# Written-out loops, and a multiply-add, an add and a relu in place of a test and a multiply, in a fused vision-and-text block on one core

## The chip, the core and the metric

The kernel runs on one core of a Trainium2 chip. Its engines are TensorE (PE; its weight loads are listed apart as PEld), VectorE (DVE), ScalarE (ACT), GpSimd (POOL) and SyncE (SP), which issues all DMAs here. Each engine has its own program and its own queue, and they wait for one another by semaphores. The metric is the device time of one launch in microseconds, median of the runs; lower is better. Before the change it is 5894.83 us.

## What is computed

For each of 8 images a tokenizer turns 518x518 pixels into 1024 tokens of width 128; 77 text tokens are appended, so L = 1101. An attention with 8 heads of width 64 and a causal mask follows, and then a second attention with 8 heads of width 16, in which every row keeps only its 16 largest logits:

```python
h = concatenate([tok(x), txt], axis=1)              # (8, 1101, 128)
h = h + causal_attn(layernorm(h))                   # softmax over tril, 8 heads x 64, plus its input
h = h + sparse_attn(layernorm(h))
# sparse_attn, after x + depthwise conv(x) and the projections of q, k, v (8 heads x 16):
logits = einsum('bmd,bpd->bmp', q * scale, k)
_, idx = lax.top_k(logits, 16)
attn = softmax(einsum('bmd,bmkd->bmk', q * scale, gather(k, idx)), axis=-1)
out = einsum('bmk,bmkd->bmd', attn, gather(v, idx)) @ wo_w.T + wo_b
```

Softmax over 16 chosen logits equals exp over all 1101 of them, set to zero where the logit isn't chosen, divided by the sum of what is left. The kernel does it so, with no gather.

## The kernel before

**Stages.** The program is a pipeline over images. Stage c (0 to 8) does the tokens and the causal attention of image c and the sparse attention of image c - 1. So stage 0 has causal work alone, stages 1 to 7 have both, and stage 8 has sparse work alone. A stage with both runs `tokens(c)`, five calls of `a_round`, `output(c)` and `projections(c)`. A round p (0 to 3) takes two heads of each attention in 18 steps, one step for each row tile of 128 tokens (9 tiles, 2 heads). The steps' order on PE and ACT is a list written out by hand (`step_events`). The last two steps' leftovers are carried into the next round, so rounds 1 to 3 begin with work of the round before.

**A sparse tile, engine by engine.** PE computes the logits into PSUM (L620). DVE takes the 8 largest (L1100), negates the first for the exp (L1105), replaces the 8 in a copy `A` by NEG (L1116), takes the next 8 (L1120) and replaces those by NEG too (L1125). ACT computes `E1 = exp(logits - max)` (L892). POOL turns `A` into a 0/1 mask by a test for NEG (L510) and multiplies it with `E1` in place (L515). Two steps later PE transposes `A` in blocks of 128 columns (L600, in groups of four into one of two PSUM banks), ACT copies each group to `PT` (L839, and L842 for the last block, 77 wide), PE sums `PT` with the values (L701), ACT copies these sums (`split`, L862) and PE joins them (L709). ACT's exp of a tile stands behind the `split` copy in ACT's queue, and PE's logits of the next tile wait for that exp.

**A causal tile.** PE computes scores (L672, with the mask added in PSUM at L680 or L667), DVE takes the row maximum (L1064), ACT the exp into `PB` (L903). PE transposes `PB` (L600 as well), the same two lines copy it (slot 1 of `PT`), and PE sums it with the values (L727).

**Loops and registers.** Stages 1 to 7 are one loop over c (a `Fori`), and within each stage rounds 1 and 2 and 3 are a loop over p, on every engine. Round 0 stands before that loop, written out. Stage 0 and stage 8 stand outside the loop over c, but their rounds 1 to 3 are loops too. In a loop the values that semaphores are compared with, and some addresses, come from registers, computed by register instructions in each engine's queue. PE's inner loop of stages 1 to 7 closes at L795, its loop over c at L791, those of stages 0 and 8 at L787 and L802.

**hold.** Many waits go through `hold`, which waits and then increments a counter that nobody waits for in the rounds.

Of the kernel before, what the change touches and what calls it, by code (L numbers as in the profile page):

```python
# [29 lines left out]
NP = HA // 2  # L30
HF, DF = 8, 16
TOK_EPS, EPS = 1e-3, 1e-5
NEG = -3.0e38
MASK = -1.0e9
# [129 lines left out]
def build(nc, x, txt, conv_w, conv_b, gamma, beta, dense_w, dense_b, W_in, b_in, W_out, b_out,  # L164
# [7 lines left out]
    with ctx:  # L172
# [167 lines left out]
        def hold(eng, s, value, counter):  # L340

            eng.wait_ge(s, value)
            eng.sem_inc(counter, 1)  # L343

# [7 lines left out]
        def _(sp):  # L352
# [64 lines left out]
            def cycle(c, first, last):  # L417

                sp.wait_ge(h_free, c + 1)
                sp.dma_start(H[0:TXT, NT - 1, :], txt[c]).then_inc(txt_loaded, 16)  # L420
                with sp.Fori(0, NP) as p:

                    sp.wait_ge(wp_free, c * NP + (p + 1))
                    for s in range(3):
                        sp.dma_start(Wp[:, s, :, :], win_v[p, s]).then_inc(wp_loaded, 16)
# [15 lines left out]
            cycle(0, True, False)  # L441
            with sp.Fori(1, B - 1) as c:
                cycle(c, False, False)
# [6 lines left out]
        def _(pool):  # L450
# [44 lines left out]
            def weights(c):  # L495


                wait_copied(pool, "FV", c - 1)
                pool.sem_inc(held_g, 1)
                with pool.Fori(0, NP) as p:  # L500
                    for k in range(STEPS):
                        if k in (0, 3):

                            hh = k // 3
                            hold(pool, weighed, sparse_tile(c, p, hh * NT) + 1, held_g)
                            nc.gpsimd.tensor_copy(Vh[:, hh, :, 0:DF + 1], Vf[:, :, 2 * p + hh, :]
                                                  ).then_inc(v_ready, 1)

                        hold(pool, cut16, sparse_tile(c, p, k) + 1, held_g)
                        nc.gpsimd.tensor_scalar(A[:, k % 3, :], A[:, k % 3, :], NEG, None, ALU.is_equal  # L510
                                                ).then_inc(marked, 1)

                        pool.wait_ge(logit_free, sparse_tile(c, p, k) + 2)
                        hold(pool, marked, sparse_tile(c, p, k) + 1, held_g)
                        nc.gpsimd.tensor_tensor(A[:, k % 3, :], A[:, k % 3, :], E1[:, k % 2, 0:L], ALU.mult  # L515
                                                ).then_inc(chosen, 1)

            halos(0)
            with pool.Fori(1, B) as c:
                halos(c)  # L520
                weights(c)
# [15 lines left out]
        def _(pe):  # L537
# [248 lines left out]
            a_round(0, 0, False, True, False)  # L786
            with pe.Fori(1, NP) as p:  # L787
                a_round(0, p, False, True, True)
            a_round(0, NP, False, True, True)
            projections(0, True)  # L790
            with pe.Fori(1, B) as c:  # L791
                tokens(c)
                sparse_inputs(c)
                a_round(c, 0, True, True, False)
                with pe.Fori(1, NP) as p:  # L795
                    a_round(c, p, True, True, True)
                a_round(c, NP, True, True, True)
                output(c)
                projections(c, False)
            sparse_inputs(B)  # L800
            a_round(B, 0, True, False, False)
            with pe.Fori(1, NP) as p:  # L802
                a_round(B, p, True, False, True)
# [5 lines left out]
        def _(act):  # L809
# [23 lines left out]

            def copy_turned(bank, slot, q0, tiles):

                short = tiles[-1] == NT - 1
                full = len(tiles) - short
                if full:
                    last = nc.scalar.copy(PT[:, slot, 128 * q0:128 * (q0 + full)], bank[:, 0:128 * full])  # L839
                if short:  # L840
                    o = 128 * (q0 + full)
                    last = nc.scalar.copy(PT[0:LAST, slot, o:o + 128], bank[0:LAST, 128 * full:128 * full + 128])  # L842
                last.then_inc(turn_free, 1)
# [90 lines left out]
            a_round(0, 0, False, True, False)  # L934
            with act.Fori(1, NP) as p:
                a_round(0, p, False, True, True)
            a_round(0, NP, False, True, True)
            projections(0)
            with act.Fori(1, B) as c:
                tokens(c)  # L940
                a_round(c, 0, True, True, False)
                with act.Fori(1, NP) as p:
                    a_round(c, p, True, True, True)
# [3 lines left out]
            a_round(B, 0, True, False, False)  # L947
            with act.Fori(1, NP) as p:
                a_round(B, p, True, False, True)
# [5 lines left out]
        def _(dve):  # L955
# [221 lines left out]
            a_round(0, 0, False, True, False)  # L1177
            with dve.Fori(1, NP) as p:
                a_round(0, p, False, True, True)
            a_round(0, NP, False, True, True)  # L1180
            projections(0)
            with dve.Fori(1, B) as c:
                tokens(c)
                a_round(c, 0, True, True, False)
                with dve.Fori(1, NP) as p:
                    a_round(c, p, True, True, True)
# [3 lines left out]
            a_round(B, 0, True, False, False)  # L1190
            with dve.Fori(1, NP) as p:
                a_round(B, p, True, False, True)
# [25 lines left out]
```

## Time and profile before

| | |
|---|---|
| median of 3 runs | 5894.83 us (5883.47 to 5908.94) |
| profiled execution, from first to last instruction | 5921.3 us |
| mean granted TensorE clock | 0.855 |
| PE busy | 4872.7 us, 82% |
| DVE busy | 4044.9 us, 68% |
| POOL busy | 3189.5 us, 54% |
| ACT busy | 2745.0 us, 46% |
| stage 0 | to about 612 us |
| stages 1 to 7 | to about 5459 us, some 690 us each |
| stage 8 | to the end, about 460 us |

Of the profiled execution the page gives the span; no other time of it is known, and the span is above all three runs. A busy share is an average over the stages, and a wait counts only where the waiting engine is the one that everything else waits for. A granted clock of 1.00 stands for 2.4 GHz and 0.50 for 1.2 GHz; values between are mixtures over time. In the timeline an entry in brackets is the engine's idle time just before the instruction and what ended it; "issue" means that nothing that the profile shows was waited for.

### The profile page before, as it was taken

To read this page: it belongs to the slowest core of one execution; us is meant where nothing else is said; L and a number is where in the kernel's file an instruction comes from. 1 tells how busy PE (TensorE), PEld (TensorE's weight loads), DVE (VectorE), ACT (ScalarE), POOL (GpSimd) and SP (SyncE) were. 2 spreads that over 40 slices of the span, in tenths; PEclk is the share of its full clock that TensorE was granted. 3 is DMA by queue.
4 is the path that set the end of the run, shared out by engine and by line. 5 is a ranking of instruction groups with operands and counts; after the bars stand their busy time and mean duration, and the time that the engine had idled before them with its cause. 6 is when DMAs were issued, how large, how long until landed. Compare 5 with 4: busy or idle time off the path is not lost. (4 is left out here: it accounts for less than half of the span.)

```text
span 5921.3 us, 104393 instructions
## 1 busy us (share of the span) xinstructions
PE 4872.7 (82%) x33480; PEld 3298.2 (56%) x33928; DVE 4044.9 (68%) x6958; ACT 2745.0 (46%) x5521; POOL 3189.5 (54%) x1495
## 2 busy tenths in 40 slices
PE   5999699887988688886998879886988879884777
PEld 3666565555555555564555645555555555553444
DVE  1111487766888488775778578884878668883887
ACT  1222255544555355553555445552555435552444
POOL 1000176653766176663666357661767447762887
PEclk8555798998999899898889989997999989996666
DMA  3020301003020300103020120203010030003000
GB/s 49 2 28 0 47 3 29 3 5 48 3 30 2 51 2 9 24 5 48 2 30 2 28 26 3 30 2 52 3 22 9 5 48 3 3 2 48 1 0 4
DMA packets 221648, 104.95 MB, mean 18 GB/s; under 512 B 183616, under 2 KB 198544, under 8 KB 221072
## 3 DMA queue, kind: packets, MB, share of 16 engines
q1 hardware_dynamic: 221072, 97.68, 11.1%
q8 instruction: 311, 5.10, 0.4%
q14 instruction: 265, 2.17, 0.1%
HBM read 78.98 MB, written 18.67 MB: 16 GB/s over the span
## 5 line engine op out<-in xcount | busy, mean ns | idle before, releaser
L510 POOL TENSOR_SCALAR A<-A 128x1101 f32<-128x1101 f32 x576 | 1732.6, 3008 | 1652.8 <-DVE A L1125 1651.6
L839 ACT COPY PT<-causal_ps 128x512 f32<-128x512 f32 (+3 forms) x1984 | 1064.8, 561 | 1216.9 <-PE causal_ps L600 1213.3
L515 POOL TENSOR_TENSOR A<-A,E 128x1101 f32<-128x1101 f32 x576 | 1378.8, 2394 | 101.6 <-POOL A L510 98.3
L1100 DVE MAX8 top<-logit_ps 128x8 f32<-128x1101 f32 x576 | 753.9, 1309 | 546.6 <-PE logit_ps L620 544.2
L600 PE MATMUL causal_ps<-ident,A 128*128 128x128 f32 (+1 forms) x5184 | 926.6, 313 | 18.2 <-POOL A L515 17.7
L727 PE MATMUL out_ps<-qk,PT 128*128 128x64 f32 x5760 | 875.7, 300 | 24.4 <-ACT PT L839 24.0
L672 PE MATMUL causal_ps<-qk 64*128 64x512 f32 (+3 forms) x1792 | 864.7, 596 | 11.7 <-ACT PB L903 6.6
L727 PEld LDWEIGHTS out_ps<-qk,PT 128*128 128x128 f32 x5760 | 808.7, 215 | 81.9 <-ACT PT L839 35.4
L1120 DVE MAX8 top<-A 128x8 f32<-128x1101 f32 x576 | 753.4, 1308 | 83.8
L600 PEld LDWEIGHTS causal_ps<-ident,A 128*128 128x128 f32 (+1 forms) x5184 | 693.2, 162 | 206.9 <-issue 148.7
L701 PE MATMUL out_ps<-PT,Vh 128*32 128x128 f32 (+1 forms) x10368 | 763.0, 302 | 38.8 <-DVE O L1088 14.9
L1116 DVE MATCH_REPLACE8 A<-top,logit_ps 128x1101 f32<-128x1101 f32 x576 | 746.1, 1295 | 0.0
L1125 DVE MATCH_REPLACE8 A<-top,A 128x1101 f32<-128x1101 f32 x576 | 743.5, 1291 | 0.0
L892 ACT ACTIVATE E<-logit_ps,negtop 128x1101 f32<-128x1101 f32 x576 | 686.9, 1193 | 61.7 <-DVE A L1116 60.7
L842 ACT COPY PT<-causal_ps 77x128 f32<-77x128 f32 x640 | 167.5, 262 | 854.6 <-PE causal_ps L600 854.0
L600 PE MATMUL causal_ps<-ident,PB 128*128 128x128 f32 (+1 forms) x2880 | 539.6, 307 | 0.0
L620 PE MATMUL logit_ps<-stack 128*128 (+2 forms) x1280 | 308.1, 334 | 251.2 <-ACT E L892 105.0
L1064 DVE TENSOR_REDUCE negmax<-causal_ps 128x1 f32<-128x128 f32 (+7 forms) x512 | 374.9, 743 | 161.9 <-PE causal_ps L680 161.9
L672 PEld LDWEIGHTS causal_ps<-qk 64*128 64x128 f32 x1792 | 324.0, 207 | 282.8 <-issue 256.5
L701 PEld LDWEIGHTS out_ps<-PT,Vh 128*32 128x32 f32 (+1 forms) x10368 | 271.5, 112 | 354.2 <-issue 186.6
L903 ACT ACTIVATE PB<-causal_ps,negmax 128x1024 f32<-128x1024 f32 (+7 forms) x576 | 454.9, 791 | 20.7 <-DVE negmax L1064 20.7
L709 PE MATMUL out_ps<-join,split 128*128 128x17 f32 x1152 | 240.8, 285 | 257.5 <-ACT split L862 257.5
(140 smaller groups left out, 3931.3 us busy)
## 6 DMA issues: line engine op xcount, KB each, us to landing
stack<-qk_parts SPq DMA_DIRECT2D x128, 288.0 KB, 20.2
X<-in_x SPq DMA_DIRECT2D x248, 121.5 KB, 4.1
qk_parts<-O SPq DMA_DIRECT2D x16, 864.0 KB, 4.8
Wp<-in_L_attn_W_in SPq DMA_DIRECT2D x96, 64.0 KB, 2.0
out<-OUTB SPq DMA_DIRECT2D x8, 512.0 KB
stack<-in_L_tok_conv_w SPq DMA_DIRECT2D x30, 64.0 KB, 2.4
X<-in_x SPq DMA_DIRECT2D x8, 108.0 KB
H<-in_txt SPq DMA_DIRECT2D x8, 38.5 KB
```

The costliest lines, as they stand in the source:

```text
L510: nc.gpsimd.tensor_scalar(A[:, k % 3, :], A[:, k % 3, :], NEG, None, ALU.is_equal).then_inc(marked, 1)
L515: nc.gpsimd.tensor_tensor(A[:, k % 3, :], A[:, k % 3, :], E1[:, k % 2, 0:L], ALU.mult).then_inc(chosen, 1)
L600: last = nc.tensor.transpose(bank[0:w, 128 * j:128 * j + 128], src, ident[:, :])
L672: last = nc.tensor.matmul(score_ps[:, c0:c1], q, qk[rows, 1, c0 - HALF * j:c1 - HALF * j], start=True, stop=not diagonal)
L701: last = nc.tensor.matmul(split_sums[32 * q:32 * q + 32, :], Vh[0:rows, h % 2, k, :], PT[0:rows, 0, 128 * k:128 * k + 128], start=(k < 4), ...
L727: last = nc.tensor.matmul(causal_sums[:, o:o + DK], PT[0:rows, 1, 512 * j + 128 * q:512 * j + 128 * q + 128], Vp[0:rows, k, DK * hh:DK * h ...
L839: last = nc.scalar.copy(PT[:, slot, 128 * q0:128 * (q0 + full)], bank[:, 0:128 * full])
L892: nc.scalar.activation(E1[:, n % 2, 0:L], logit_ps[:, 0:L], ACT.Exp, bias=negtop[:, n % 3:n % 3 + 1], scale=1.0).then_inc(logit_free, 1)
L1100: nc.vector.max(top[:, s, 0:8], logit_ps[:, 0:L]).then_inc(top8, 1)
L1116: nc.vector.match_replace(A[:, s, :], top[:, s, 0:8], logit_ps[:, 0:L], NEG).then_inc(cut8, 1)
L1120: nc.vector.max(top[:, s, 8:16], A[:, s, :]).then_inc(top16, 1)
L1125: nc.vector.match_replace(A[:, s, :], top[:, s, 8:16], A[:, s, :], NEG).then_inc(cut16, 1)
```

## The change

Four things are changed together.

- **Loops.** Every `Fori` of all five engines becomes a Python loop, so each queue is one straight piece of code. All semaphore values and addresses become constants, and the register instructions and branches are gone. PE's program grows from 1620 to 7943 printed rows.
- **hold** only waits; its increment is dropped.
- **The mask on POOL.** NEG becomes -2^127. The test `A == NEG` (one operation) becomes `A * 2^-27 + (-2^100)` (two operations in one instruction): exactly 0 where `A` is NEG, and -2^100 elsewhere. The multiplication with `E1` becomes an addition: `E1` where chosen, about -2^100 elsewhere.
- **The relu on ACT.** `copy_turned` now issues `activation` with Relu for slot 0 (sparse), which turns the large negative numbers into 0, and with Copy for slot 1 (causal).

```diff
-NEG = -3.0e38
+NEG = -2.0 ** 127
+FAR = -2.0 ** 100
...
             eng.wait_ge(s, value)
-            eng.sem_inc(counter, 1)
...
-                        nc.gpsimd.tensor_scalar(A[:, k % 3, :], A[:, k % 3, :], NEG, None, ALU.is_equal
+                        nc.gpsimd.tensor_scalar(A[:, k % 3, :], A[:, k % 3, :], FAR / -NEG, FAR, ALU.mult, ALU.add
                                                 ).then_inc(marked, 1)
...
-                        nc.gpsimd.tensor_tensor(A[:, k % 3, :], A[:, k % 3, :], E1[:, k % 2, 0:L], ALU.mult
+                        nc.gpsimd.tensor_tensor(A[:, k % 3, :], A[:, k % 3, :], E1[:, k % 2, 0:L], ALU.add
                                                 ).then_inc(chosen, 1)
...
             def copy_turned(bank, slot, q0, tiles):
+                kept = ACT.Relu if slot == 0 else ACT.Copy
...
-                    last = nc.scalar.copy(PT[:, slot, 128 * q0:128 * (q0 + full)], bank[:, 0:128 * full])
+                    last = nc.scalar.activation(PT[:, slot, 128 * q0:128 * (q0 + full)], bank[:, 0:128 * full], kept)
...
-                    last = nc.scalar.copy(PT[0:LAST, slot, o:o + 128], bank[0:LAST, 128 * full:128 * full + 128])
+                    last = nc.scalar.activation(PT[0:LAST, slot, o:o + 128], bank[0:LAST, 128 * full:128 * full + 128], kept)
...
-            with pe.Fori(1, B) as c:
+            for c in range(1, B):
                 tokens(c)
                 sparse_inputs(c)
                 a_round(c, 0, True, True, False)
-                with pe.Fori(1, NP) as p:
+                for p in range(1, NP):
                     a_round(c, p, True, True, True)
```

The other loops of SP, POOL, ACT and DVE are changed in the same way.

**PE at the end of a round's loop.** The order of PE's queue, in the kernel before, where the loop over p of stages 1 to 7 closes (an ISA row here is a register instruction):

```order
L720 ISA
L605 REGISTER_ALU [waits sum_free]
L727 MATMUL out_ps<-qk,PT 128x64 [waits turn_free]
L727 MATMUL out_ps<-qk,PT 128x64 x3
L795 REGISTER_ALU
L795 COMPARE_AND_BRANCH
```

The branch leads back to the loop's head, which reads:

```order
L620 ISA [waits logit_free]
L620 REGISTER_ALU
L620 MATMUL logit_ps<-stack 128x512
L620 ISA
L620 MATMUL logit_ps<-stack 128x512
L620 ISA
L620 MATMUL logit_ps<-stack 128x77
L605 ISA
L727 MATMUL out_ps<-qk,PT 128x64 [waits turn_free]
L727 MATMUL out_ps<-qk,PT 128x64 x3
```

The same place in the changed kernel, from the last sums of a round into the first logits of the next:

```order
L727 MATMUL out_ps<-qk,PT 128x64 x3
L620 MATMUL logit_ps<-stack 128x512 [waits logit_free]
L620 MATMUL logit_ps<-stack 128x512
L620 MATMUL logit_ps<-stack 128x77
L727 MATMUL out_ps<-qk,PT 128x64 [waits turn_free]
L727 MATMUL out_ps<-qk,PT 128x64 x3
```

The matmuls keep their order; the branch and the register instructions are gone, and the wait for the exp sits on the matmul itself.

**ACT near the end of a round.** ACT's queue in the kernel before, in a step with both kinds of work:

```order
L839 COPY PT<-causal_ps 128x512 [waits turn_done]
L850 REGISTER_ALU
L886 COPY tail<-causal_ps 128x77 [waits turn_done]
L850 REGISTER_ALU
L842 COPY PT<-causal_ps 77x128 [waits turn_done]
L850 REGISTER_ALU
L839 COPY PT<-causal_ps 128x512 [waits turn_done]
L862 COPY split<-out_ps 128x128 [waits split_done]
L889 REGISTER_ALU
L892 ACTIVATE E<-logit_ps,negtop 128x1101 [waits cut8,chosen]
```

And in the changed kernel:

```order
L840 ACTIVATE PT<-causal_ps 128x512 [waits turn_done] x2
L887 COPY tail<-causal_ps 128x77 [waits turn_done]
L843 ACTIVATE PT<-causal_ps 77x128 [waits turn_done]
L840 ACTIVATE PT<-causal_ps 128x512 [waits turn_done]
L863 COPY split<-out_ps 128x128 [waits split_done]
L893 ACTIVATE E<-logit_ps,negtop 128x1101 [waits cut8,chosen]
```

The order is the same; every copy into `PT` has become an ACTIVATE instruction, those of the causal work too, while `tail` and `split` stay COPY. ACT's whole queue holds one ACT_TABLE_LOAD in either kernel.

## Rows read from the trace of the kernel before

**Rows 1.** Busy time by stretch: bounds, length, engines, clock, DMA share, GB/s.

```profile
111.00:612.00 501.00, 461.94 (x1561) 310.15 (x1560) 85.81 (x232) 133.46 (x306) 4.71 (x32) 0.55 0.07 9
...
2887.00:3041.00 154.00, 139.71 (x915) 91.13 (x928) 117.29 (x189) 77.37 (x162) 97.73 (x38) 0.83 0.01 3
...
4935.00:5072.00 137.00, 121.16 (x930) 79.33 (x944) 116.80 (x188) 77.77 (x166) 98.21 (x39) 0.99 0.01 3
...
5569.00:5680.00 111.00, 85.46 (x562) 51.35 (x569) 98.85 (x130) 49.95 (x90) 97.40 (x37) 0.62 0.00 1
```

**Rows 2.** Waits of PE: who waited for whom, us in total, times, longest.

```profile
PE out_ps L709 <- ACT split L862: 257.5, 576, 0.5
...
PE logit_ps L620 <- ACT E L892: 105.0, 109, 4.6
PE logit_ps L620 <- issue: 61.5, 92, 3.4
...
PE out_ps L727 <- ACT PT L839: 24.0, 43, 1.0
PE causal_ps L600 <- POOL A L515: 17.7, 31, 1.7
...
PE causal_ps L666 <- ACT PT L839: 13.3, 56, 0.2
```

**Rows 3.** Timeline at the close of a round's loop, stage 3: start, us, engine, line.

```profile
2485.96 1.20 ACT L892 ACTIVATE E<-logit_ps,negtop 128x1101 f32<-128x1101 f32 x1
...
2486.84 1.00 PE L727 MATMUL out_ps<-qk,PT 128*128 128x64 f32 x8
...
2490.80 0.41 PE L620 MATMUL logit_ps<-stack 128*128 x2 [2.96 <-issue]
...
2491.05 1.50 PE L727 MATMUL out_ps<-qk,PT 128*128 128x64 f32 x8
```

**Rows 4.** Timeline of ACT: last and first causal exp around two changes of round, stage 3.

```profile
2199.72 1.10 ACT L903 ACTIVATE PB<-causal_ps,negmax 128x1024 f32<-128x1024 f32 x1
...
2223.53 0.37 ACT L903 ACTIVATE PB<-causal_ps,negmax 128x128 f32<-128x128 f32 x1 [0.29 <-DVE negmax L1064]
...
2487.88 1.10 ACT L903 ACTIVATE PB<-causal_ps,negmax 128x1024 f32<-128x1024 f32 x1
...
2516.27 0.37 ACT L903 ACTIVATE PB<-causal_ps,negmax 128x128 f32<-128x128 f32 x1 [0.30 <-DVE negmax L1064]
```

**Rows 5.** Timeline of a step of stage 3, from the last sparse sums to the join.

```profile
2595.07 0.41 PE L701 MATMUL out_ps<-PT,Vh 77*32 77x128 f32 x2
2595.17 0.59 ACT L839 COPY PT<-causal_ps 128x512 f32<-128x512 f32 x1 [0.68 <-PE causal_ps L600]
...
2595.98 0.40 PE L709 MATMUL out_ps<-join,split 128*128 128x17 f32 x2 [0.51 <-ACT split L862]
```

**Rows 6.** Groups of instructions by line: busy us, mean ns, idle before, releaser.

```profile
L510 POOL TENSOR_SCALAR A<-A 128x1101 f32<-128x1101 f32 x576 | 1732.6, 3008 | 1652.8 <-DVE A L1125 1651.6
L515 POOL TENSOR_TENSOR A<-A,E 128x1101 f32<-128x1101 f32 x576 | 1378.8, 2394 | 101.6 <-POOL A L510 98.3 <-ACT E L892 2.5 <-issue 0.9
...
L868 ACT ACTIVATE qk<-causal_ps,bqkv 128x1024 f32<-128x1024 f32 x32 | 35.7, 1115 | 91.9 <-PE causal_ps L630 91.9
...
L872 ACT COPY qk<-causal_ps 128x1024 f32<-128x1024 f32 x32 | 32.4, 1012 | 50.3 <-PE causal_ps L636 50.3
```

**Rows 7.** Timeline of stage 8: DVE and POOL from tile to tile.

```profile
5700.40 1.30 DVE L1100 MAX8 top<-logit_ps 128x8 f32<-128x1101 f32 x1
...
5706.20 1.30 DVE L1100 MAX8 top<-logit_ps 128x8 f32<-128x1101 f32 x1
...
5706.47 3.02 POOL L510 TENSOR_SCALAR A<-A 128x1101 f32<-128x1101 f32 x1
...
5712.28 3.01 POOL L510 TENSOR_SCALAR A<-A 128x1101 f32<-128x1101 f32 x1
```

**Rows 8.** Timeline of stage 3's tokens: the second layernorm.

```profile
2060.81 1.84 DVE L992 BATCH_NORM_STATS2 st<-H 128x6 f32<-128x128 f32 x9 [12.91 <-DMA H<-in_txt]
```

More of the change, by code:

```diff
@@ L420, in cycle @@
                 sp.dma_start(H[0:TXT, NT - 1, :], txt[c]).then_inc(txt_loaded, 16)
-                with sp.Fori(0, NP) as p:
+                for p in range(0, NP):
                     sp.wait_ge(wp_free, c * NP + (p + 1))
@@ L441, in _ @@
             cycle(0, True, False)
-            with sp.Fori(1, B - 1) as c:
+            for c in range(1, B - 1):
                 cycle(c, False, False)
@@ L499, in weights @@
                 pool.sem_inc(held_g, 1)
-                with pool.Fori(0, NP) as p:
+                for p in range(0, NP):
                     for k in range(STEPS):
@@ L514, in weights @@
                         hold(pool, marked, sparse_tile(c, p, k) + 1, held_g)
-                        nc.gpsimd.tensor_tensor(A[:, k % 3, :], A[:, k % 3, :], E1[:, k % 2, 0:L], ALU.mult
+                        nc.gpsimd.tensor_tensor(A[:, k % 3, :], A[:, k % 3, :], E1[:, k % 2, 0:L], ALU.add
                                                 ).then_inc(chosen, 1)
             halos(0)
-            with pool.Fori(1, B) as c:
+            for c in range(1, B):
                 halos(c)
@@ L790, in _ @@
             projections(0, True)
-            with pe.Fori(1, B) as c:
+            for c in range(1, B):
                 tokens(c)
@@ L794, in _ @@
                 a_round(c, 0, True, True, False)
-                with pe.Fori(1, NP) as p:
+                for p in range(1, NP):
                     a_round(c, p, True, True, True)
@@ L801, in _ @@
             a_round(B, 0, True, False, False)
-            with pe.Fori(1, NP) as p:
+            for p in range(1, NP):
                 a_round(B, p, True, False, True)
@@ L934, in _ @@
             a_round(0, 0, False, True, False)
-            with act.Fori(1, NP) as p:
+            for p in range(1, NP):
                 a_round(0, p, False, True, True)
@@ L938, in _ @@
             projections(0)
-            with act.Fori(1, B) as c:
+            for c in range(1, B):
                 tokens(c)
                 a_round(c, 0, True, True, False)
-                with act.Fori(1, NP) as p:
+                for p in range(1, NP):
                     a_round(c, p, True, True, True)
@@ L947, in _ @@
             a_round(B, 0, True, False, False)
-            with act.Fori(1, NP) as p:
+            for p in range(1, NP):
                 a_round(B, p, True, False, True)
@@ L1177, in _ @@
             a_round(0, 0, False, True, False)
-            with dve.Fori(1, NP) as p:
+            for p in range(1, NP):
                 a_round(0, p, False, True, True)
@@ L1181, in _ @@
             projections(0)
-            with dve.Fori(1, B) as c:
+            for c in range(1, B):
                 tokens(c)
                 a_round(c, 0, True, True, False)
-                with dve.Fori(1, NP) as p:
+                for p in range(1, NP):
                     a_round(c, p, True, True, True)
@@ L1190, in _ @@
             a_round(B, 0, True, False, False)
-            with dve.Fori(1, NP) as p:
+            for p in range(1, NP):
                 a_round(B, p, True, False, True)
```

## Prediction

> **What bounds the kernel now.** I read the stages first. PE is the engine to follow in stages 1 to 7: in a round of some 137 us it is busy 121 us at a clock of 0.99 [rows 1], while DVE, ACT and POOL are busy 117, 78 and 98 us. Stage 0 is PE too, at a clock of 0.55 and 92% busy [rows 1]. In stage 8 PE (85 of 111 us, clock 0.62), DVE (99) and POOL (97) are close together [rows 1]. So a microsecond counts in stages 0 to 7 if PE stands idle in it, and in stage 8 if it is taken from all three.
>
> Then PE's waits [rows 2]: 257.5 us before the join L709 for ACT's `split`, 105.0 us before the logits L620 for ACT's exp, 61.5 us before L620 with "issue", where nothing was waited for. Between images there is a second limit: the layernorm of the tokens waits 12.91 us for the text's DMA [rows 8], which stands in SP's queue behind the loads of `stack`. What makes PE quicker there is swallowed by that wait.
>
> **Loops written out.** At the close of the loop over p, PE ends L727 at 2487.84, the exp that L620 needs was over at 2487.16, and still L620 starts at 2490.80 [rows 3]: 2.96 us lost on the branch. Right behind it the same eight L727 take 1.50 us instead of 1.00 [rows 3]: the clock has fallen to its lower level (1.2 GHz) after the pause. The whole price is read by comparing two changes of round with the same work. From round 0 to round 1, where no branch is taken back, the last causal exp of a round and the first of the next lie 2223.53 - 2199.72 = 23.81 us apart; from round 2 to round 3 it is 2516.27 - 2487.88 = 28.39 us [rows 4]. I read all of stages 1 to 7 in this way: the 7 changes without the branch have 23.80 to 23.81 us, the 14 with it 28.08 to 30.19, mean 29.06. So 14 x (29.06 - 23.80) = **74 us** go. The loop over c closes 6 times with a pause of PE as well, but the wait for the text ends later [rows 8], so I count nothing; without that cover it would be about 2 us each, 12 in all. In stages 0 and 8 the branches show no such pause.
>
> **Registers and holds.** Of the 61.5 us of "issue" [rows 2], 14 x 2.96 = 41 are counted already. The rest, 20 us, are logits whose wait sat on a register instruction; I take 15. Where L620 waits for the exp, that instruction costs about 0.1 us more than a direct wait (0.15 us from the exp's end against 0.05 at L709 from `split`'s); 39 of the 109 waits lie before stage 8: 4 us. Elsewhere PE's and DVE's register instructions run ahead of the work: stage 0's written-out round and its looped rounds have the same length within 1%. Together **19 us** in stages 1 to 7.
>
> **POOL.** L510 costs 3.01 us, L515 2.39 us [rows 6]. No row has a multiply-add on POOL. From below, a two-input multiply of the same size costs 2.39; from above, two operations for one may double it, 6.02. I take 3.01, since it is the same instruction on the same tile, and the add like the multiply. In stages 1 to 7 POOL is idle a quarter of the time and PE waits for it 17.7 us in all [rows 2], 14.2 of them in stage 8, so nothing changes there for anything up to about 4.7 us.
>
> The Trainium skill (GPSIMD Engine Reference, section 3.1) says that a body with at most two operations per element is bound by its port at 1.03 cycles; an estimate by it is 1101 x 1.03 / 1.2 GHz = 0.95 us plus dispatch. By that, POOL's tile would fall from 5.8 to about 3.8 us and the sum would stay as it is, because DVE holds stage 8 at nearly the same pace. The trace bears such low figures out badly: one operation takes 3.01 us [rows 6].
>
> **ACT.** Each copy into `PT` becomes an ACTIVATE. The nearest rows, same shape and source: ACTIVATE 1115 ns, COPY 1012 ns [rows 6]. I take +0.10 us each; the range is 0 (if Relu and Copy are leaner than the biased form) to 0.10 on more of them than I count. No second table load is in the queue. ACT isn't full, so only exposed copies count. In most steps of stages 1 to 7 a causal copy stands before `split`: PE's sums L701 end at 2595.48, the copy at 2595.76, and L709 waits 0.51 us [rows 5]. I counted 306 of 504 joins with a wait of about 0.5 us, 114 with about 0.4 and 84 at the floor of 0.35: 306 x 0.10 + half of 114 x 0.10 = 36 us. L666 waits 56 times and L727 43 times for L839 [rows 2]: 10 us. A few L701: 4 us. Together **+50 us**. This is the term that speaks against the change.
>
> **Stage 8.** DVE goes from tile to tile in 5.80 us and POOL in 5.81 [rows 7]; the mean over the tiles is 111 / 18 = 6.2 [rows 1], since the loop through PE and ACT is slower when the clock is low. The written-out round 0 has 14 tiles in 84.5 us, rounds 1 to 3 in 86.7: 3 x 2.8 = 8 us for 18 tiles each. The dropped increments of `hold` shorten DVE's two gaps of 0.15 us and POOL's of 0.17 us by some 0.1 each: 8 us over the tiles that they bind. L620's direct wait gives 70 x 0.1 = 7 us, the slower ACT takes some 8 back. **-15 us**.
>
> **Sum.** 5921.3 - 74 - 19 + 50 - 15 = 5863 us for the profiled span, a factor of 0.990. The span is above the runs, so I apply the factor to the median: 5894.83 x 0.990 = **5837 us**.
>
> **Rivals.**
>
> *The clock moves more than the branch.* In steps 3 to 7 of a round PE's work is thin, and the clock falls there in most rounds, for 14 to 44 us. Round 1 of stage 4 took 154 us at 0.83, round 1 of stage 7 137 us at 0.99 [rows 1]: 17 us between worst and best. Against the best round all of them together lose 134 us. Shorter pauses should keep the clock up more often; if half of it goes, 5837 - 67 = 5770. The other way, if 10 more rounds are as bad as the worst, 6000. I see a reason for the first only, in the pauses that shrink by 0.1 us.
>
> *Only the pause goes.* The clock falls at the change of round all the same, so of 74 us only 41 come, and the slower copies are exposed about 20 us more, in the turn of the two PSUM banks. 5837 + 33 + 20 = 5890.
>
> *Code loading.* Straight code is longer than any loop body, and under the burst of `stack` loads a small transfer is late: the text's ends a wait of 12.91 us [rows 8]. If PE's code came as late in 7 stages by some 10 us, 5907. Against it: the code of stages 1 to 7 that isn't looped, tokens and round 0, is read the same way today, without a pause there. The Trainium skill (Runtime: NRT & Kernel Launch, Instruction fetch mechanics) calls sequential fetching mostly hidden and a taken branch a stall; by it this rival gives nothing and the sum stays.
>
> *POOL becomes the bound (slower than before).* If two operations cost twice the time, a tile on POOL takes 6.02 + 2.39 + 0.3 = 8.7 us, against 7.8 us per tile in stages 1 to 7 and 6.2 in stage 8. 504 x 0.9 + 72 x 2.5 = 634 us more than 5921, scaled about 6530. It decides from L510 above 3.3 us in stage 8 and above 4.7 us in the others (7.4 after the change, less 2.7).
>
> **How the numbers follow.** The forecast, 0.50, with a range of its own of 5800 to 5870. Half of the clock's loss gone, 0.20: 5770. Only the pause, 0.16: 5890. Code loading, 0.04: 5907. POOL, 0.06: 6530. Clock worse, 0.04: 6000. The range from 5750 to 5900 leaves out 0.10 above and a little below: if the copies cost nothing more and half of the clock's loss goes too, it is 5837 - 50 - 67 = 5720. Some 0.5% is what a measurement of this kernel can tell from no change; that is under 5865 for faster and over 5924 for slower. Faster holds the forecast nearly whole, the clock's gain and a part of the third case: 0.76. Same: 0.13. Slower: 0.11.
>
> **What would show it.** Right: no "issue" wait of more than 1 us before L620, changes of round of 24 us everywhere in stages 1 to 7, L839's 512 columns at 0.69 us instead of 0.59, L709's waits up by 0.1 us in three of five steps, L510 within 2.4 to 3.3 us. Wrong: PE idle with "issue" in straight code; POOL ending PE's waits before L600; round lengths that change in steps 3 to 7 with the clock, which would outweigh each of my terms.

## The result, and the profile after

The changed kernel takes **5693.2 us** in the median (5677.7 to 5703.7, 4 runs), the kernel before 5893.5 beside it. The ratio is 0.965, with a 95% interval of 0.960 to 0.970: faster by 200 us, where I had forecast 58, and outside my range (5750 to 5900). A second set of runs on another chip gave 0.964 [0.958, 0.970].

The profiled execution took 5677.7 us with a span of 5675.9. The span before was above all its runs, so the two spans differ by 245 us, more than the medians do. The account of the spans by part of the program:

| part, us | before | after |
|---|---|---|
| stage 0, first to last causal exp | 474.8 | 474.6 |
| 28 rounds of stages 1 to 7, first to last causal exp | 3214.6 | 3114.9 |
| 21 changes of round in stages 1 to 7 | 573.5 | 487.0 |
| between the stages | 961.3 | 952.3 |
| stage 8 with what leads into it | 576.9 | 527.4 |
| stretches at the low clock that touch the 28 rounds | 382 | 177 |

The first 120 us of each span, the same within 0.5 us, are not in the table. Of the low stretches 372 and 172 us lie inside the rounds.

The waits of PE after the change (who waited for whom, us in total, times, longest) answer to [rows 2]:

```profile
PE out_ps L709 <- ACT split L863: 259.4, 576, 0.5
...
PE logit_ps L620 <- ACT E L893: 101.3, 106, 4.3
...
PE out_ps L727 <- ACT PT L840: 25.9, 43, 0.8
...
PE logit_ps L620 <- issue: 16.4, 84, 0.2
```

"Issue" before L620 fell from 61.5 to 16.4 us, and its longest from 3.4 to 0.2: the pause at the branch is gone. The waits for the join hardly moved. At the same place as [rows 3], a close of a round in stage 3, the timeline now reads:

```profile
2400.82 1.00 PE L727 MATMUL out_ps<-qk,PT 128*128 128x64 f32 x8
2401.88 0.41 PE L620 MATMUL logit_ps<-stack 128*128 128x512 bf16 x2
2402.13 0.85 PE L727 MATMUL out_ps<-qk,PT 128*128 128x64 f32 x6
```

L620 follows at once, and the L727 behind it run at full clock.

The stretches (bounds, length, busy time of PE, PEld, DVE, ACT, POOL, clock, DMA share, GB/s) answer to [rows 1]: stage 0, an undisturbed round of stage 4, the slowest round of all (stage 4 too), and stage 8.

```profile
111.00:594.00 483.00, 443.21 (x1467) 294.46 (x1465) 84.64 (x228) 126.76 (x297) 4.71 (x32) 0.55 0.06 10
```

```profile
2812.00:2923.00 111.00, 101.05 (x777) 66.17 (x790) 99.74 (x163) 65.34 (x141) 54.00 (x32) 0.98 0.00 1
...
2946.00:3070.00 124.00, 114.81 (x775) 75.95 (x789) 99.00 (x161) 65.66 (x140) 53.94 (x32) 0.85 0.27 33
...
5562.00:5673.00 111.00, 81.47 (x591) 51.15 (x599) 90.46 (x122) 50.32 (x90) 60.10 (x36) 0.74 0.00 1
```

Stage 0 is as before, clock and all. In stage 8 POOL is busy 60 us of 111 instead of 97. DVE alone sets the pace there, 5.43 us from tile to tile (5302.61 to 5308.04), with POOL waiting for it:

```profile
5302.61 1.30 DVE L1101 MAX8 top<-logit_ps 128x8 f32<-128x1101 f32 x1
...
5308.04 1.30 DVE L1101 MAX8 top<-logit_ps 128x8 f32<-128x1101 f32 x1
```

```profile
5302.78 1.11 POOL L510 TENSOR_SCALAR A<-A 128x1101 f32<-128x1101 f32 x1 [1.65 <-DVE A L1126]
```

Last, the groups by line and shape (busy us, mean ns, idle before) for the changed operations, against [rows 6] and, for the copy, its own row of before:

```profile
L510 POOL TENSOR_SCALAR A<-A 128x1101 f32<-128x1101 f32 x576 | 642.2, 1115 | 2493.5 <-DVE A L1126 2493.5
```

```profile
L840 ACT ACTIVATE PT<-causal_ps 128x512 f32<-128x512 f32 x1664 | 939.0, 596 | 954.1 <-PE causal_ps L600 954.0
```

```profile
L839 ACT COPY PT<-causal_ps 128x512 f32<-128x512 f32 x1664 | 931.7, 588 | 1086.6 <-PE causal_ps L600 1083.4
```

The multiply-add takes 1.115 us where the test took 3.008, and the ACTIVATE 0.008 us more than the COPY.

### The profile page after: what moved, and what is told of

It is laid out like the page before. It is cut to its first block, busy times and chain, and to the rows that moved or that the text cites. A ratio compares the mean times of both kernels' runs of the same rounds, so it can differ in the third digit from the quotient of the medians.

```text
span 5675.9 us, 86247 instructions
## 1 busy us (share of the span) xinstructions
PE 4706.9 (83%) x33480; PEld 3201.5 (56%) x33928; DVE 4020.6 (71%) x6958; ACT 2745.6 (48%) x5521; POOL 2101.8 (37%) x1495
## 4 chain that ended last, share of the span: by engine, by line
PE 69%; DVE 10%; ACT 10%; DMA 5%; issue 4%; SPq 2%; POOL 0%; POOLq 0%; ACTq 0%; DVEq 0%
PE causal_ps L600 18%; PE causal_ps L672 14%; PE out_ps L727 13%; PE out_ps L701 7%; PE logit_ps L620 4%; ACT PT L840 4%; DMA H<-in_txt 4%; PE out_ps L709 3%; PE causal_ps L630 2%; ACT split L863 2%; DVE top L1101 2%; DVE A L1126 2%; PE causal_ps L680 1%; DVE top L1121 1%; DVE A L1117 1%
## 5 line engine op out<-in xcount | busy, mean ns | idle before, releaser
L840 ACT ACTIVATE PT<-causal_ps 128x512 f32<-128x512 f32 (+3 forms) x1984 | 1075.9, 569 | 1072.2 <-PE causal_ps L600 1071.8
L510 POOL TENSOR_SCALAR A<-A 128x1101 f32<-128x1101 f32 x576 | 642.2, 1115 | 2493.5 <-DVE A L1126 2493.5
L727 PE MATMUL out_ps<-qk,PT 128*128 128x64 f32 x5760 | 852.5, 294 | 27.0 <-ACT PT L840 25.9
L600 PE MATMUL causal_ps<-ident,A 128*128 128x128 f32 (+1 forms) x5184 | 867.4, 299 | 3.6 <-POOL A L515 1.5
L672 PE MATMUL causal_ps<-qk 64*128 64x512 f32 (+3 forms) x1792 | 842.0, 582 | 11.1 <-ACT PB L904 6.6
L727 PEld LDWEIGHTS out_ps<-qk,PT 128*128 128x128 f32 x5760 | 789.4, 211 | 82.8 <-issue 51.7
L701 PE MATMUL out_ps<-PT,Vh 128*32 128x128 f32 (+1 forms) x10368 | 744.6, 294 | 32.6 <-ACT PT L840 10.5
L600 PEld LDWEIGHTS causal_ps<-ident,A 128*128 128x128 f32 (+1 forms) x5184 | 646.8, 154 | 173.5 <-issue 142.7
L843 ACT ACTIVATE PT<-causal_ps 77x128 f32<-77x128 f32 x640 | 174.6, 273 | 802.8 <-PE causal_ps L600 802.5
L620 PE MATMUL logit_ps<-stack 128*128 128x512 bf16 (+1 forms) x1280 | 293.3, 320 | 197.2 <-ACT E L893 101.3
L701 PEld LDWEIGHTS out_ps<-PT,Vh 128*32 128x32 f32 (+1 forms) x10368 | 267.1, 110 | 331.2 <-issue 157.4
```

Source lines behind the costliest of these rows:

```text
L510: nc.gpsimd.tensor_scalar(A[:, k % 3, :], A[:, k % 3, :], FAR / -NEG, FAR, ALU.mult, ALU.add).then_inc(marked, 1)
L600: last = nc.tensor.transpose(bank[0:w, 128 * j:128 * j + 128], src, ident[:, :])
L672: last = nc.tensor.matmul(score_ps[:, c0:c1], q, qk[rows, 1, c0 - HALF * j:c1 - HALF * j], start=True, stop=not diagonal)
L701: last = nc.tensor.matmul(split_sums[32 * q:32 * q + 32, :], Vh[0:rows, h % 2, k, :], PT[0:rows, 0, 128 * k:128 * k + 128], start=(k < 4), ...
L727: last = nc.tensor.matmul(causal_sums[:, o:o + DK], PT[0:rows, 1, 512 * j + 128 * q:512 * j + 128 * q + 128], Vp[0:rows, k, DK * hh:DK * h ...
L840: last = nc.scalar.activation(PT[:, slot, 128 * q0:128 * (q0 + full)], bank[:, 0:128 * full], kept)
```

## The experiments

Ratios are to the kernel before on the same chip, with their 95% interval. Line numbers shift by one or two where an edit adds lines. A clock fall is counted in the step in which it begins. Steps are numbered from 0, as in the kernel, and step n is here the time from the last causal exp of step n - 1 to the first of step n.

### The loops, by engine

Four kernels are the kernel before with loops written out, and nothing else changed: on all engines, on PE, on all but PE, and on DVE.

```diff
-                with pe.Fori(1, NP) as p:
+                for p in range(1, NP):
```

All engines:

> The kernel before with all loops of all engines written out and nothing else: the test and multiply on POOL, the copies on ACT and the increments of hold stay. Theory L (the written-out loops give the time, by the pauses and register instructions that go, and by a clock that no longer falls in steps 3 to 7): of the 200 us at least 140, so a median of 5710 to 5755, round lengths of stages 1 to 7 mostly 109 to 112 us, stage 8 back by 15 us or less. Theory P (the quicker POOL gives what I missed): only the changes of round and the registers go, 5894 - 93 = about 5800, falls of the clock in steps 3 to 7 as before. If it is below 5700, loops alone do all of it and the arithmetic nothing.

PE alone:

> The kernel before with the loops of PE alone written out. If PE's own pauses and register instructions are the cause (my prediction's view, with the clock's gain added): changes of round of 23.8 us everywhere in stages 1 to 7, and a median of 5730 to 5810. If the registers and loops of the others matter as much (DVE stands 78 us with issue before L1088, POOL and ACT have pauses of their own at the change of round): 5830 to 5860, with changes of round of 25 us or more.

All but PE:

> The kernel before with the loops of SP, POOL, ACT and DVE written out and PE's kept. If PE's own branch and registers are the cause: 5880 to 5900, changes of round of 28 to 30 us. If the other engines' register instructions are: 5780 to 5830. A sum rule: the gains of this kernel and of the one with PE's loops alone should add up to that of all loops written out; if they add up to clearly more, either of them removes the same stall, if to less, both are needed.

DVE alone:

> The kernel before with the loops of DVE alone written out. All engines but PE gave 51 us (0.9913), with the changes of round unchanged at 577 us. DVE stands with issue before L1088 for 78 us in the kernel before, each time with PE's L701 waiting for it next (14.9 us in all), and 1 us when written out. If DVE is the one of the four that matters: 5830 to 5850 and PE's wait for L1088 under 1 us. If POOL and ACT share in it: 5860 to 5880.

| loops written out on | median us | ratio | changes of round | 28 rounds |
|---|---|---|---|---|
| all | 5722.7 | 0.973 [0.968, 0.977] | 492.3 | 3109.1 |
| PE | 5806.6 | 0.985 [0.978, 0.991] | 501.7 | 3172.8 |
| all but PE | 5833.0 | 0.991 [0.989, 0.994] | 577.6 | 3116.0 |
| DVE | 5817.8 | 0.986 [0.982, 0.991] | 577.9 | 3119.7 |

PE's loops give back the changes of round, 573.5 - 501.7 = 72 us, and some of the rounds. The other half of the gain is DVE's alone, and it lies in the rounds: 3214.6 - 3119.7 = 95 us. That is the part that I had priced at nothing. DVE's output of the causal sums (L1088) before, and with DVE's loops written out:

```profile
L1088 DVE TENSOR_SCALAR O<-out_ps,rinv 128x64 f32 (+1 forms) x576 | 157.6, 283 | 366.8 <-PE out_ps L727 273.8 <-issue 78.4 <-DVE rinv L1077 10.9
```

```profile
L1088 DVE TENSOR_SCALAR O<-out_ps,rinv 128x64 f32<-128x64 f32 x576 | 157.7, 283 | 276.3 <-PE out_ps L727 275.8 <-issue 0.3
```

DVE stood 78.4 us with nothing to wait for. In a case of stage 3 three register instructions fill such a gap of 0.27 us, with 85, 107 and 64 ns, and with DVE's loops written out there is none. No run removes the register instructions of this line alone, so that these matter among DVE's is argued and not shown. PE's sparse sums L701 wait for L1088 to free the PSUM; in the kernel before

```profile
PE out_ps L701 <- DVE O L1088: 14.9, 44, 0.4
```

and with DVE's loops written out

```profile
PE out_ps L701 <- DVE O L1088: 0.3, 1, 0.3
```

A round in which the clock never falls is 109.0 to 109.2 us long with DVE's loops written out and 109.5 to 110.2 before, some 22 us over 28 rounds, of which these waits are 15. The rest of the 95 us goes with the clock: the low stretches that touch the rounds sum to 382 us before and to 188 here. PE and DVE add up: 0.0154 + 0.0138 = 0.029, against 0.0275 for all. All engines but PE give less than DVE alone, 0.9% against 1.4%, but the two intervals overlap and their rounds have the same length. Theory L of the first expectation holds. For all but PE I had 5780 to 5830 and for DVE alone 5830 to 5850; the one came out 3 us above and the other 12 below.

### The arithmetic alone

The kernel before with its loops and its hold, and multiply-add, add and relu as in the change:

> The kernel before with its loops and its hold, and only the arithmetic changed: multiply-add and add on POOL, relu in ACT's copy. Theory P: 5894 - 110 = about 5785, with fewer falls of the clock in stages 1 to 7. Theory L: only stage 8 gains, where POOL (5.81 us a tile) no longer holds DVE, 72 tiles x 0.2 to 0.4 us = 15 to 30 us, and the copies into PT cost 0.01 us more, about 5 us: 5865 to 5885; changes of round still 29 us.

**6091.8 us, 1.032 [1.027, 1.037]: slower by 3%.** Neither theory had this sign. The 28 rounds take 3416.6 us instead of 3214.6. The timeline shows a 128x1 instruction that takes 1.52 us (stage 5, round 2, step 11):

```profile
3925.48 1.11 POOL L511 TENSOR_SCALAR A<-A 128x1101 f32<-128x1101 f32 x1 [3.74 <-DVE A L1127]
...
3926.76 2.53 POOL L516 TENSOR_TENSOR A<-A,E 128x1101 f32<-128x1101 f32 x1 [0.17 <-POOL A L511]
...
3927.78 1.52 DVE L1076 TENSOR_TENSOR rowsum<-rowsum 128x1 f32<-128x1 f32 x1
...
3930.37 0.31 DVE L1134 TENSOR_TENSOR X<-out_ps,rden 128x144 f32 x1
...
3930.81 0.43 PE L702 MATMUL out_ps<-PT,Vh 128*32 128x128 f32 x8 [1.39 <-DVE X L1134]
```

DVE's add of two row sums ends at 3929.30, and so does POOL's add, at 3929.29. Behind it `normalise` (L1134) is late, and PE stands 1.39 us for it. The same spot in the kernel before:

```profile
3800.84 3.01 POOL L510 TENSOR_SCALAR A<-A 128x1101 f32<-128x1101 f32 x1 [1.82 <-DVE A L1125]
...
3803.14 0.14 DVE L1074 TENSOR_TENSOR rowsum<-rowsum 128x1 f32<-128x1 f32 x1
...
3804.01 2.52 POOL L515 TENSOR_TENSOR A<-A,E 128x1101 f32<-128x1101 f32 x1 [0.17 <-POOL A L510]
```

Here the add meets POOL's test, and is not held. I took all 64 adds of each trace apart. Before: 7 begin during POOL's TENSOR_TENSOR and take 1.15 us, 35 begin during its TENSOR_SCALAR and 22 while POOL is idle, all of these 0.14 to 0.16 us. With the new arithmetic 35 begin during the TENSOR_TENSOR and end 0.014 to 0.020 us behind it. With the quicker multiply-add, POOL's second operation slides under DVE's add.

The Trainium skill (SBUF — State Buffer, Who interferes with whom) says that a VectorE instruction with two SBUF inputs contends with a GpSimd one that reads SBUF, that the ports they share are an exclusive lock, and that the order of issue decides which of the two is blocked. By that, the adds during TENSOR_TENSOR agree to 0.02 us; those during POOL's test, which reads SBUF too, do not.

What PE's pause costs is in the windows of four steps (step 10's second exp to step 14's), before and with the new arithmetic:

```profile
3801.78:3828.48 26.70, 23.88 (x192) 15.53 (x195) 24.46 (x43) 15.30 (x35) 20.79 (x8) 1.00 0.01 2
```

```profile
3925.92:3964.35 38.43, 34.93 (x189) 22.14 (x189) 26.90 (x44) 15.67 (x35) 13.69 (x8) 0.64 0.00 1
```

The clock fell 2.3 us after the pause and stayed low for 27.3 us. Of the 64 low stretches that touch the rounds 25 begin in step 11, with 580 of 812 us. PE's waits for `normalise` in all, before and with the new arithmetic:

```profile
PE out_ps L701 <- DVE X L1132: 5.7, 16, 1.3
```

```profile
PE out_ps L702 <- DVE X L1134: 46.4, 42, 2.3
```

Two kernels take the meeting away, from either side. The first keeps everything and gives DVE's add one SBUF input and a per-partition scalar:

```diff
-                        step(nc.vector.tensor_tensor(rowsum[:, s, 0:1], rowsum[:, s, 0:1], rowsum[:, s, 1:2],
-                                                     ALU.add))
+                        step(nc.vector.tensor_scalar(rowsum[:, s, 0:1], rowsum[:, s, 0:1], rowsum[:, s, 1:2],
+                                                     None, ALU.add))
```

> The kernel before with loops and hold, the arithmetic changed on POOL and ACT as in the run of the arithmetic alone (6091.84 us), and one more edit: DVE's add of the two row sums (L1074, 128x1, two inputs in SBUF) is written as a tensor_scalar, whose second value is a per-partition scalar. Theory S (that add is held up until POOL's add L515 ends, up to 1.67 us, in 35 of 64 cases; normalise and with it PE are late, and the clock falls for the steps behind it): the add takes 0.14 to 0.2 us everywhere, PE's waits for normalise fall from 46 us to under 6, rounds 1 to 3 of stages 1 to 7 are 110 to 115 us instead of 124, and the time is 5850 to 5890. Theory R (register instructions and a different order of arrivals make the loops slow with a quick POOL, whatever DVE's add does): above 6000. Theory H (the add is held up in either form): 6090.

5889.4 us, 0.998 [0.994, 1.001]: at the upper end of theory S. PE's waits for `normalise` fall to 11.7 us and not to under 6, and no fall begins in step 11. The add takes 0.20 us in the middle of POOL's operation:

```profile
3761.02 2.52 POOL L516 TENSOR_TENSOR A<-A,E 128x1101 f32<-128x1101 f32 x1 [0.17 <-POOL A L511]
...
3762.04 0.20 DVE L1076 TENSOR_SCALAR rowsum<-rowsum 128x1 f32<-128x1 f32 x1
```

The second leaves DVE alone and has POOL do one operation instead of two, so that it ends sooner:

```diff
-NEG = -2.0 ** 127
-FAR = -2.0 ** 100
+NEG = -2.0 ** 100
...
-                        nc.gpsimd.tensor_scalar(A[:, k % 3, :], A[:, k % 3, :], FAR / -NEG, FAR, ALU.mult, ALU.add
-                                                ).then_inc(marked, 1)
...
-                        nc.gpsimd.tensor_tensor(A[:, k % 3, :], A[:, k % 3, :], E1[:, k % 2, 0:L], ALU.add
+                        nc.gpsimd.tensor_tensor(A[:, k % 3, :], A[:, k % 3, :], E1[:, k % 2, 0:L], ALU.mult
...
-                kept = ACT.Relu if slot == 0 else ACT.Copy
+                kept, scale = (ACT.Relu, 1.0 / NEG) if slot == 0 else (ACT.Copy, 1.0)
```

> The kernel before with its loops, its hold and DVE's add as it was, and the arithmetic with one operation on POOL (NEG is -2^100, POOL multiplies A by E1, ACT's relu takes a scale of -2^-100). POOL's operation on A starts and ends 1.1 to 1.3 us earlier than in the kernel with the arithmetic alone (6092 us), so DVE's add meets only its last 0.3 us or nothing. Theory S (the meeting of the two costs the 200 us): 5870 to 5900 us, TensorE's waits for normalise under 10 us. Theory R (a quick POOL in the loops is slow by itself): 6050 or more.

5898.5 us, 1.002 [0.998, 1.006]. The adds take 0.43 us at most, and PE waits 13.4 us for `normalise`, where I had said under 10. The times of both agree with theory S: one 128x1 instruction, held 35 times, cost 200 us, most of it through the clock (low stretches of 812 us against 382).

ACT's part of the change by itself (the copies as ACTIVATE with Copy, in the kernel before):

> The kernel before with ACT's copies into PT as ACTIVATE with the function Copy, nothing else. My prediction's term says +0.10 us for each and +50 us in all: 5940. The trace of the changed kernel has them only 0.008 to 0.012 us longer: 5890 to 5900, or, if the 0.01 us shifts arrivals enough to bring a few falls of the clock, up to 5910.

5897.6 us, 1.003 [0.999, 1.006]: about nothing, and not the 50 us of my sum.

### Is it the pause, or the registers?

Three kernels put a pause into the changed kernel, whose loops are written out. They have the tensor_scalar add, and ahead of it at step 11 reductions of a constant that nobody reads: 1024 columns, 1024 + 640, or 1024 + 1024.

```diff
+                    if n == 9 and sparse:
+                        nc.vector.reduce_max(junk[:, 4 * c + p:4 * c + p + 1], cols[:, 0:1].broadcast_to((128, 1024)), AX.X)
```

> The changed kernel with DVE's add of the row sums as a tensor_scalar, and right ahead of it, once in each round of stages 1 to 7 (step 11), a reduction over 1024 columns of a constant that nobody reads: 28 delays of some 1.1 to 1.3 us on DVE, the size of the hold-up in the kernel with the arithmetic alone. If the 198 us lost there come from the delay of PE at that step (PE waits 1.4 us for normalise, the clock falls, 25 falls at that step make 580 us at the low clock), this kernel loses in the same way: 28 x 1.3 = 36 us at least, and 150 to 200 us with the clock, 5850 to 5920. If a delay alone doesn't bring the clock down, and the loops' register instructions are needed too: 5718 + 36 = 5755 or less.

> As the run with one delay on DVE at step 11 (5691.68 us, TensorE's pause before L701 0.65 us), with a second constant reduction of 640 columns behind the first, some 0.8 us more: TensorE should stand about 1.4 us there, as in the kernel with the arithmetic alone. Theory G (the pause of TensorE alone brings the clock down, and one of 0.65 us doesn't while one of 1.4 us does): low-clock stretches of 27 us or more begin in that step in most of the 28 rounds, steps 11 to 13 take 9 us instead of 6.3, some 8 us a round: 28 x (0.8 + 8) = 246, 5900 to 5960 us. Theory J (the loops' register instructions are needed too): no falls there, 5692 + 28 x 0.8 = 5715.

> The same with a second reduction of 1024 columns, 1.2 us: TensorE should stand about 1.85 us. Theory G: as with the smaller dose, 11 us more: 5910 to 5975 us. Theory J: 5692 + 28 x 1.2 = 5726. If only this dose brings the clock down, the step from harmless to harmful lies between 1.4 and 1.85 us in this kernel.

PE's waits for DVE in the three, in this order:

```profile
PE out_ps L702 <- DVE O L1092: 18.2, 28, 0.9
```

```profile
PE out_ps L702 <- DVE O L1093: 38.8, 28, 1.4
```

```profile
PE out_ps L702 <- DVE O L1093: 50.0, 28, 1.8
```

| delay on DVE | PE's pause | rounds with a fall in step 11 | low clock from these | median us | ratio |
|---|---|---|---|---|---|
| none | 0 | 0 of 28 | 0 us | 5718.0 | 0.967 [0.960, 0.973] |
| 1.2 us | 0.65 us | 0 of 28 | 0 us | 5691.7 | 0.965 [0.962, 0.969] |
| 2.0 us | 1.38 us | 23 of 28 | 140 us | 5818.8 (see below) | 0.988 [0.978, 0.998] |
| 2.4 us | 1.79 us | 28 of 28 | 304 us | 5893.0 | 0.998 [0.995, 1.002] |

The four runs with 1.38 us lie in two pairs, at 5768 and 5778 us and at 5859 and 5870, so their median says little. The trace is of the run of 5768; what made the second pair longer no trace shows, and I count with the first. Its median, 5773, is 81 us above the kernel with 0.65 us, and in the traces the rounds are 63 us longer; 28 x 0.73 = 20 are the pause itself. From 1.38 to 1.79 us the rounds grow by another 87 us, of which 11 are the pause. So a pause of PE brings the clock down with no register instruction near. My three numbers were all off: I had expected the first dose to do it, the second to cost as much as in the loops (5900 to 5960), and the third 5910 to 5975. There most falls last 27.3 us, here 6.8 us, and only with the longest pause do some last 30.7 or 41.0. What makes a fall last long, I can't say from these runs. A window of four steps after a pause of 1.38 us, and the worst one after 1.79:

```profile
3849.95:3879.61 29.66, 26.50 (x191) 17.03 (x191) 26.21 (x44) 15.12 (x35) 13.23 (x8) 0.88 0.01 1
```

```profile
4164.70:4206.57 41.87, 38.66 (x190) 23.28 (x188) 28.20 (x46) 15.89 (x35) 14.09 (x8) 0.56 0.00 1
```

### Inside the changed kernel

The same kernel once more, with the old arithmetic, with hold's increments put back, with the tensor_scalar add, and with one operation on POOL (diffs as above; the increment is the line `eng.sem_inc(counter, 1)`).

> The changed kernel itself once more, so that it stands on the same chip as the next three: 5680 to 5710 us. Its trace tells how far the places where the clock falls repeat: in the first trace 12 of 25 falls in stages 1 to 7 begin at a change of round and last 3.4 or 13.7 us, and four begin near the 10th step and make up 82 of 177 us at the low clock. If these places belong to the program, they come again; if not, the split over the steps is chance and only the sum counts.

> The changed kernel with the old arithmetic (test and multiply on POOL, COPY on ACT): loops written out and the increments of hold gone. Against all loops written out with the increments (5722.67 us) it shows what the increments cost, against the changed kernel what the arithmetic gives. Expected by the account of the parts: stage 8 is bound by POOL (3.01 + 2.39 + gaps of 0.17 and less), so about 5.6 us a tile there, 405 to 425 us for the 72 tiles instead of 432 and 396; stages 1 to 7 as in either. 5705 to 5720. If the increments give nothing: 5723; if they give all of the difference: 5693.

> The changed kernel with the increments of hold back in. By the account of stage 8 (period 5.71 us with increments, 5.43 us without, POOL not binding) it loses 72 x 0.28 = 20 us there, less where the clock holds a tile, and 0.1 us in the thin steps of stages 1 to 7, 28 x 6 x 0.1 = 17 us if these are bound by DVE: 5700 to 5715. If the increments cost nothing: 5675 to 5693.

> The changed kernel (5693.2 us) with DVE's add of the two row sums as a tensor_scalar. Theory S: the add takes 0.87 to 1.22 us in 33 of 64 cases now and 0.14 to 0.2 then; the step in which it stands (the 10th of a round, mean 6.64 us) goes to 6.05, 28 x 0.6 = 17 us, and a clock fall or two less: 5665 to 5680. If the delay is covered by other work in this kernel: 5693 within 0.3%.

> A version of the changed kernel with one operation on POOL for a tile instead of two: NEG is -2^100, POOL multiplies A by E1 (E1 is at most 1, so this is -2^100 times E1 where chosen), and ACT's relu takes a scale of -2^-100, which gives E1 back where chosen and practically 0 elsewhere. L510 and its 1.11 us are gone, POOL is busy 1380 us instead of 2100, and A is ready 1.3 us earlier. If the held-up add of DVE matters, it ends 1.3 us earlier, mostly before DVE comes to it. Stage 8 is held by DVE at 5.43 us a tile already, so little comes there, under 10 us. 5670 to 5690; if nothing waits for A or the add, the same as the changed kernel.

| changed kernel | median us | ratio | stage 8 | PE's L701 for L1089 |
|---|---|---|---|---|
| as it is, again | 5675.5 | 0.964 [0.958, 0.970] | 527.3 | 0.8 us |
| with the old arithmetic | 5731.7 | 0.969 [0.962, 0.976] | 560.6 | 0.0 |
| with hold's increments | 5761.4 | 0.978 [0.974, 0.983] | 548.9 | 25.2 |
| with the tensor_scalar add | 5718.0 | 0.967 [0.960, 0.973] | 531.2 | 0.0 |
| with one operation on POOL | 5704.9 | 0.967 [0.963, 0.971] | 532.1 | 0.0 |

Stage 8 is settled: the arithmetic gives 560.6 - 527.3 = 33 us there, the increments' absence 22 with the new arithmetic and 10 with the old (571.0 - 560.6). Outside it the rounds are 55 us longer with the increments, and I put most of that down to the same meeting, though no run with the increments and the tensor_scalar add tests it. With the increments, DVE's add is longer and PE waits:

```profile
L1076 DVE TENSOR_TENSOR rowsum<-rowsum 128x1 f32<-128x1 f32 x64 | 44.1, 689 | 0.0
```

```profile
PE out_ps L702 <- DVE O L1090: 25.2, 42, 1.0
```

Seven falls begin in step 11 there, and none or one in the changed kernel, whose add is held as well:

```profile
L1075 DVE TENSOR_TENSOR rowsum<-rowsum 128x1 f32<-128x1 f32 x64 | 35.3, 552 | 0.0
```

In the changed kernel the add is held to 0.87 to 1.22 us in 33 of 64 cases, mostly without PE noticing. Removing that, by either edit, gives nothing; the intervals of these two kernels and of the changed one overlap. Four of my five forecasts here were too low, by 12 us (old arithmetic), 46 (increments), 38 (tensor_scalar add) and 15 (one operation); in these four the clock is low for 233 to 289 us inside the rounds, against 172 in the changed kernel. My 17 us for the tensor_scalar add did come in step 11 (6.64 us in the mean, then 6.03), and went again in steps 3 to 6, where the clock was low for 208 us instead of 3. Why it falls there more often I can't say. No version here beats the changed kernel.

The places of the falls belong to the program, not to chance: on another chip the changed kernel had 26 low stretches that touch its rounds instead of 25, and 75 us low from those of step 9 instead of 82.

## Why the prediction was wrong, step by step

- **The changes of round: right.** I said -74 us; PE's loops alone gave -72, the change in all -86.5. All intervals are now 23.1 us but one.
- **"PE's and DVE's register instructions run ahead of the work": this step failed.** I tested it on stage 0 alone, where DVE is busy for 86 of 501 us [rows 1], and left DVE's 78 us of "issue" before L1088 out of the sum. With DVE's loops written out they were worth 71 us (5888.7 to 5817.8), as much as PE's branch. The term of 19 us had left out DVE. That it is DVE's loops is shown; that it is the registers of L1088 among them is argued.
- **The clock: the rival was right, for another reason.** I gave the loss in the rounds' thin steps a chance of 0.20, and "pauses that shrink by 0.1 us" as its cause. The low stretches went from 382 to 177 us, and the rounds lost 100 us against my 67 for that case. Written-out loops of DVE alone bring 95 of the 100 and 382 down to 188 (PE's alone 42), so the cause is DVE's loops, in the main.
- **ACT's copies, +50 us: mis-sized.** I took 0.10 us for each from the rows of a biased ACTIVATE [rows 6]; measured were 0.008 to 0.012, and nothing in the time. The difference of 0.10 in [rows 6] is not that of ACTIVATE and COPY. The Trainium skill (ScalarE: Activation LUTs, What ACT_TABLE_LOAD costs) gives 93 ns to a per-partition bias operand; the trace agrees, 103 ns with the bias and 8 without.
- **POOL's multiply-add: outside my bounds.** I took 3.01 us between 2.39 and 6.02; it is 1.115. A one-operation row of another kind was no bound at all. The estimate beside it by the Trainium skill (GPSIMD Engine Reference, section 3.1), 0.95 us plus dispatch, was right, and I set it aside since the test's 3.01 us spoke against it.
- **Stage 8, -15 us: mis-sized.** It lost 50. Mine held the new pace at POOL's 5.8 us; with 1.115 us POOL leaves the chain, and DVE without the increments needs 5.43. The loops gave 6 of this, the increments 10, the arithmetic 33.
- **What I saw nowhere: the parts do not add.** The arithmetic is +3.2% with the loops (by DVE's held add), +0.6% with loops written out and increments (0.973 to 0.978, intervals that overlap), and -0.4% without them (0.969 to 0.965, within their intervals). That it costs nothing in the changed kernel was luck as far as my forecast goes: I saw neither the hold nor that the steps around that add mostly cover it there. Outside stage 8 the arithmetic gave the change nothing that stands clear of the intervals.

The sum of the misses in the spans: 50 (ACT) + 35 (stage 8) + 81 (rounds, 100 less 19) + 12 (changes of round) + 9 (between the stages, not taken apart) = 187, which is 245 - 58. The medians differ by 45 less than the spans, and 187 - 45 = 142 is what the forecast was off, 5837 against 5693, but for rounding.

## What to carry to other kernels

Read "issue" waits on every engine that frees something for the engine that bounds, not on that engine alone, and ask of each what it makes late. Before an operation on GpSimd is made quicker, look which two-input VectorE instructions with SBUF operands it will now run against: a 128x1 add can be held for 1.5 us. Where TensorE's pauses come near a microsecond, price a change by the pauses that it makes and not by its sum of durations.

## What the hardware showed unexpectedly

- A VectorE TENSOR_TENSOR from SBUF that begins during a GpSimd TENSOR_TENSOR stands until that is over (up to 1.9 us, with PE's loops alone written out), and isn't held by a GpSimd test for equality that runs as long (0.14 to 0.16 us in all of 242 cases, over seven traces).
- On GpSimd two operations in one instruction (multiply, add) took 1.115 us on 128x1101, one test for equality 3.008.
- Pauses of TensorE of 1.38 us, 28 of them, made the rounds 63 us longer in the traces than pauses of 0.65 us, where the pauses themselves account for 20; those of 0.65 us brought no fall of the clock in their step.
- At the close of the loop over p in stages 1 to 7 TensorE paused 2.6 to 3.4 us, 14 times. The clock fell each time: in the kernel before 5 times within the pause and 9 times 0.2 to 1.2 us behind it, with the loops of DVE or of all engines but PE written out 14 of 14 times within it.
